# Attention with heads of 16: the values of the last 26 keys applied by one 128x128 product of a block-diagonal matrix instead of four 128x32 column tiles

## What is computed

```python
q = (x @ Wq).reshape(B, N, 16, 16).transpose(0, 2, 1, 3)
k = (context @ Wk).reshape(B, M, 16, 16).transpose(0, 2, 1, 3)
v = (context @ Wv).reshape(B, M, 16, 16).transpose(0, 2, 1, 3)
attn = softmax(einsum('bhid,bhjd->bhij', q, k) * scale)
out = einsum('bhij,bhjd->bhid', attn, v)          # 154 keys: 128 and the last 26
x = x + tanh(gate) * (out.transpose(0, 2, 1, 3).reshape(B, N, D) @ Wo)
```

## Time and profile before

| what | value |
| --- | --- |
| median of three runs | 1677.46 us (1675.73 to 1680.3) |
| the profiled execution, whole | 1669.4 us |
| its span, first to last instruction | 1667.6 us |
| mean granted TensorE clock in it | 0.887 of full |
| TensorE, matmuls | 1318.3 us busy (79%) |
| VectorE | 684.0 us (41%) |
| ScalarE | 470.9 us (28%) |
| GpSimd | 278.2 us (17%) |

### The profile page before, as it was taken

How to read it: one execution, slowest core, us unless ns; L and a number is a source line. 1 busy time by engine, 2 the same in 40 slices (tenths; PEclk the granted TensorE clock), 3 DMA queues, 4 the chain that set the end, 5 groups by cost and what they waited for, 6 DMA issues and landing times.

```text
span 1667.6 us, 17067 instructions
## 1 busy us (share of the span) xinstructions
PE 1318.3 (79%) x6107; PEld 769.0 (46%) x6137; DVE 684.0 (41%) x1743; ACT 470.9 (28%) x877; POOL 278.2 (17%) x336
## 2 busy tenths in 40 slices
PE   5998889689978744999876499943789556899995
PEld 2544443345655522544433277731334323566663
DVE  4745245573242389754445011125414482111115
ACT  1243344212211154044421133311365220222220
POOL 5100010050000003220014300035410017000016
PEclk9799989889998967699986699976799868899997
DMA  6000010010000100100025222221000022445434
GB/s 219 1 1 1 1 48 0 5 49 1 0 0 0 27 3 1 51 1 1 1 92 205 82 64 64 67 68 53 1 1 1 1 78 94 140 134 159 134 96 139
DMA packets 73951, 86.90 MB, mean 52 GB/s; under 512 B 11026, under 2 KB 66702, under 8 KB 73742
## 3 DMA queue, kind: packets, MB, share of 16 engines
q1 hardware_dynamic: 67726, 69.04, 13.4%
q0 software_dynamic: 6144, 16.79, 3.2%
HBM read 59.71 MB, written 26.08 MB: 51 GB/s over the span
## 4 chain that ended last, share of the span: by engine, by line
PE 69%; DVE 12%; POOL 8%; issue 5%; ACT 4%; DMA 1%; SPq 0%; POOLq 0%; DVEq 0%; ACTq 0%
PE bank L1059 6%; PE bank L617 4%; PE bank L681 4%; PE bank L1031 4%; PE bank L1106 4%; PE bank L1044 4%; PE bank L599 4%; POOL x_slots L1576 4%; POOL scratch L1589 3%; PE bank L705 3%; PE bank L723 3%; PE bank L734 3%; PE bank L870 3%; PE bank L737 2%; PE bank L786 2%
## 5 line engine op out<-in xcount | busy, mean ns | idle before, releaser
L1059 PE MATMUL bank<-scratch 128*128 128x320 f32 (+3 forms) x480 | 153.7, 479 | 0.6 <-issue 0.6
L1171 ACT ACTIVATE scratch<-bank 128x512 f32<-128x512 f32 x240 | 123.4, 605 | 107.8 <-PE bank L712 79.6
L1494 POOL TENSOR_SCALAR rstd<-mv 128x4 f32<-128x4 f32 x36 | 9.8, 273 | 791.4 <-DVE mv L1609 718.4
L1793 DVE TENSOR_REDUCE scratch<-bank 128x2 f32<-128x308 f32 x256 | 105.3, 472 | 76.8 <-PE bank L681 76.3
L1589 POOL DMA_INDIRECT scratch<-y_slots,scratch x64 | 61.1, 955 | 390.4 <-DMA y_slots<-scratch 371.5
L2269 DVE TENSOR_TENSOR scratch<-scratch,bank 128x320 f32<-128x320 f32 (+3 forms) x60 | 31.5, 526 | 218.4 <-PE bank L1059 218.4
L1059 PEld LDWEIGHTS bank<-scratch 128*128 128x128 f32 (+1 forms) x480 | 87.6, 186 | 62.8 <-issue 30.7
L1140 ACT ACTIVATE scratch<-bank 128x512 f32<-128x512 f32 x56 | 31.7, 595 | 218.2 <-PE bank L557 218.0
L2162 DVE TENSOR_TENSOR scratch<-bank,weights 128x512 f32<-128x512 f32 x39 | 27.0, 691 | 153.4 <-PE bank L1031 153.4
L681 PE MATMUL bank<-scratch 32*128 32x308 f32 x512 | 85.4, 521 | 1.3 <-DVEq L1678 1.3
L1576 POOL DMA_INDIRECT x_slots<-scratch x64 | 66.1, 1033 | 71.8 <-DVEq L2256 29.0
(11 more groups left out here) (376 smaller groups left out, 2229.3 us busy)
## 6 DMA issues: line engine op xcount, KB each, us to landing
scratch<-in_L_ffn_W SPq DMA_DIRECT2D x16, 512.0 KB, 9.9
scratch<-in_L_ffn_w_gate SPq DMA_DIRECT2D x16, 352.0 KB, 4.0
scratch<-in_L_ffn_w_up SPq DMA_DIRECT2D x16, 352.0 KB, 4.4
x_slots<-zeros SPq DMA_DIRECT2D x1, 5120.0 KB, 20.8
scratch<-x_slots SPq DMA_DIRECT2D x39, 128.0 KB, 2.2
y_slots<-scratch SPq DMA_DIRECT2D x39, 128.0 KB, 1.7
scratch<-in_L_ffn_w_down SPq DMA_DIRECT2D x16, 256.0 KB, 4.5
scratch<-x_slots SPq DMA_DIRECT2D x16, 256.0 KB, 3.0
```

Source lines behind the costliest of these rows:

```text
L1059: last = pe.matmul(bk[0:fn, 0:n], w[:, s, k, m * P:m * P + fn], moving(k), start=k == 0, stop=k == DK - 1)
L1171: act.activation(v["PT"][:, n % 2, j, :], bk[:], ACT.Exp, scale=float(v["hd"]) ** -0.5).then_inc(RP.read, 1)
L1793: dve.tensor_reduce(v["mx"][:, TPC * c + t, r, 2 * m:2 * m + 2], bk[:, 0:2 * M].rearrange("p (e k) -> p e k", k=M), AX.X, ALU.max)\
```

## The change

In the step "av" the second loop of four products on 32 columns each goes, and one product takes its place, whose stationary operand is all four heads' blocks of `Vr` at once. It adds to the same bank, and it raises the semaphore that ScalarE waits for. Nothing else changes: not the order, the banks, the waits, the data or other engines.

```diff
@@ -733,10 +733,8 @@
                         for r in range(4):
                             pe.matmul(bk[32 * r:32 * (r + 1), :], v["V"][:, b, head(g, r), :],
                                       v["PT"][:, slot, r, :], start=True, stop=False)
-                        for r in range(4):
-                            last = pe.matmul(bk[32 * r:32 * (r + 1), :], v["Vr"][:, b, g, r, :],
-                                             v["PT"][:, slot, 4, :], start=False, stop=True)
-                        last.then_inc(RP.filled, 1)
+                        pe.matmul(bk[:], v["Vr"][:, b, g, :, :].rearrange("p j d -> p (j d)"), v["PT"][:, slot, 4, :],
+                                  start=False, stop=True).then_inc(RP.filled, 1)
```

## The result

The changed kernel took 1685.2 us in the median of six runs (1682.86 to 1686.03), the kernel before 1676.6 us (six runs, 1674.07 to 1680.3): a ratio of 1.0048 with a 95% interval of 1.0034 to 1.0062. That is 8.6 us slower, where the prediction had 4.6. The time lies in the range (1676 to 1688), just outside the forecast's own range (1679 to 1685), and on the slower side of the 0.3% line, to which 44 in 100 was given. The mechanism on TensorE is the forecast one, within 0.01 us for each part; the sum has one term too few, worth 1.0 us. The remaining 3 us or so are not in the steps that were changed. One execution of the kernel before, in the third set of the experiments (1727.86 us at a mean clock of 0.843), was in a slower state of the chip and is left out of every comparison.

The account below looks back on a forecast made before the run. TensorE was taken to bound the attention phases. 16 steps at 0.195 us (3.1 us) and 32 at 0.045 us (1.4 us) gave +4.6 us on the median, 1682.1 us (+0.27%); range 1676 to 1688, the forecast's own 1679 to 1685.

Parts of the forecast that it names:

- the 0.3% line: Whole kernel: smallest change a measurement can tell, here 5.0 us; slower by more had 0.44, within it 0.52.
- The bound: TensorE sets the attention phases; 47 of 48 "av" steps lie on the chain, so gains or losses reach the end time.
- The gain of merging: Second half of "av": four tiles already run together, so merging gains nothing apart from some 0.02 us of stagger.
- The rival by which removed instructions give back time: In "av", six removed passes save 0.027 us each, 7.8 us over 48 steps, giving 1674.3 us; 4 in 100.
- The boundary: Between uses of the array in "av": each change of tiling costs 0.09 us, and the next weight load shows.
- The free and the dear boundary: New boundary inside "av": free, 5.8 us less, 1671.7 us, 4 in 100; dear, 7.2 us on top, 1689.3 us, 5 in 100.
- The two kinds of steps: "av" before "max": 16 steps at 0.195 us more; before a full-array step: 32 at 0.045 us more.
- The copy: Rival: fourth head's scores wait for ScalarE's copy of "av", losing 0.15 us in 32 steps; 1686.9 us, 7 in 100.
- It decides if the fourth head's last pass moves to within 0.52 of L723: Condition for the copy to set the path; 0.61 us was said to be left in layer 3 and layers 0 and 2.
- L723's wait for ScalarE: Sign of the copy's rival: L723 would wait longer for ScalarE than 0.54 us.
- The clock: Whole kernel: +-2.5 us for granted clock and the median of a few runs; price per step hardly depends on it.

Follow-up runs that it names:

- full_first: Against the changed kernel: the full product is issued first and begins the sum, the four column tiles of V follow; ratio to the kernel before 1.0005.
- the changed kernel with pairs: Against the changed kernel: scores issued head by head, each head's f32 and bf16 products behind each other, in layers 0 and 2; ratio to the kernel before 1.0070.

## Why the prediction was right, and where it was not

**The bound.** "The chain runs through 47 of the 48 steps" and "whatever the step gains or loses goes into the end time" held: six delays of 0.86 us each came through as 0.855 to 0.860.

**The gain of merging.** "Nothing" held. The full product's passes last 0.43 us plus boundary and load, like four tiles' passes together, and full_first shows the pair at the price of before. The rival by which removed instructions give back time is out: full_first also issues six passes fewer in each step, and its intervals are those of before, where that rival wanted 6 x 0.027 = 0.16 us less each. The Trainium skill, TensorEngine Tiling (Array Packing), section Instruction Overhead, states an overhead of some 60 cycles for each matmul; for tiles that go through the array together the traces don't bear it out.

**The boundary.** Of 0.99, 1.05, 0.96 and 0.53 us the trace has 1.00, 1.06, 0.96 and 0.53. The Trainium skill, in the same page's section Tiling Modes, says that changing the tiling mode drains the engine. The trace agrees that a change costs time, 0.09 us, and adds the weight load that shows behind it (a first pass of 0.53 instead of 0.43 us); but the next pass starts 0.52 us behind one that lasts 0.59, so by these records, whose ends are modelled, it does not wait until the last result is out. The free and the dear boundary, bounds and rivals both, are out. The two kinds of steps cost +0.20 and +0.05, as in the sum.

**The copy.** The step of the reasoning that failed is "It decides if the fourth head's last pass moves to within 0.52 of L723 ... In layers 0 and 2 ... again 0.61 left". It looked for the next place where the late fourth head could hold up TensorE, and took that to be the boundary ahead of "rem". In layer 3 that is so, and the 0.61 us of slack were not used up (+0.05 per step). L723's wait for ScalarE, named as the sign of this rival, could not show it: it is 0.43 instead of 0.54 us in layer 3, and in layers 0 and 2 TensorE waits 0.54 us behind its last L712 pass in both kernels, since that pass is late by the same 0.12 us. In layers 0 and 2 the first head has a second product that stands behind the fourth head's first one in the program, and its signal comes no earlier than that one's end. There was no slack at all: ScalarE's start at 179.15 already followed the fourth L705, by 0.10 us. So the saved boundary is lost again in 8 of the 32 steps, in each of the two layers three of chunk 3 and the last of chunk 0, where only a "norm" stands between the product and the next scores, at 0.12 us each: 1.0 us. The rival's mechanism was right, its reach 8 steps instead of 32, and its size 0.12 instead of 0.15 us. The sum is 5.6 instead of 4.6 us, 0.33% instead of 0.27%, which crosses the line of 0.3%.

**The clock.** The forecast put it down as +-2.5 us of noise around the median. It is more than that, since it doesn't average out in a comparison: on one chip the changed kernel ran at a mean clock 0.0045 below that of before, its parts on another at 0.002 below (and the changed kernel with pairs at 0.007 below), and by the correlation 4 and 2 us of the measured differences go with it; on a third the clocks agreed and the difference was 6.0 us. In the first comparison 3 us of the 8.6 are not in the steps. That these are the clock's is argued from the later sets and not shown for those runs, of which only the profiled one of before has its clock on record. That the time fell inside the stated range of 12 us therefore owes something to the range's width: the steps account for 5.6 of the 8.6 us, and the forecast gave no reason for the rest. Why the kernel before had a better clock on some chips, and why every variant beside it was a little lower on two of them and hardly on the others, stays open. Delay as such was tried as the cause and did not show it on the chip where the clocks agreed, so it is not excluded for the others.

## What to carry to other kernels

Replacing four column tiles by one block-diagonal product saved no time here, where the tiles already go through the array side by side; what counted is the number of times that the array's form changes, so put a full product next to another full one. When a product waits for a bank, ask which later products in the program wait with it for their signal, however early they are done. And hold a difference of a few microseconds against the granted clock of each run before giving it to the edit.

## What the hardware showed that was not expected

A product's signal waited for products ahead of it in the program that were on other rows of the array: done at 182.61, ScalarE's start at 182.88; with the order changed, done at 179.55, start at 179.64, while the fourth head's L704, now behind it in the program, ended only at 179.71 (178.21 + 1.50). The Trainium skill, TensorE: Matmul & The Clock Gate, section Part 3: Packing small matmuls, says that matmuls both start and end in program order. The starts do not agree: that last L704 pass, of 0.59 us, began at 179.12, ahead of the first head's L707 at 179.17, which stands ahead of it in the program. Nor do all ends: the fourth head's first L704 pass ran from 178.59 to 179.28 and so ended before that L707 did (179.55), by ends that are modelled. What kept the program's order in all these steps is the signal.

At full clock a step of "av" repeats to some 0.005 us between chips, while the kernel before has medians from 1673 to 1694 us. Its two profiles have spans of 1667.6 and 1694.0 us, and their 45 intervals inside the three layers differ by 0.1 us in sum. The difference lies in the phases between.
